# Layer-0 scan of a two-layer Macaron model: the product with B and the sum over states, made per channel half or for both halves at once on GpSimd

## The reference, cut to what matters

```python
dt = softplus(dt @ dt_proj_w + dt_proj_b)        # (8, 512, 256)
A  = -exp(A_log)                                 # (256, 16)
def step(h, inp):                                # over the 512 time steps
    u_t, dt_t, B_t, C_t = inp
    dA = exp(dt_t[..., None] * A)
    h = dA * h + (dt_t * u_t)[..., None] * B_t[:, None, :]
    y = einsum('bdn,bn->bd', h, C_t)             # sum over the 16 states
    return h, y
out = (y + u * D) * silu(z) @ out_proj_w
```

## Time and profile before

| what | us |
|---|---|
| median of 3 runs | 1867.86 |
| profiled execution, span from first to last instruction | 1918.1 |
| stretch in which scans run | about 126 to 1004 |
| TensorE busy over the span | 1729.9 |
| VectorE busy | 1279.6 |
| GpSimd busy | 1210.5 |
| ScalarE busy | 1105.3 |

### The profile page before, as it was taken

How to read it: one execution, slowest core, us unless ns; L and a number is a source line. 1 busy time by engine, 2 the same in 40 slices (tenths; PEclk the granted TensorE clock), 3 DMA queues, 4 the chain that set the end, 5 groups by cost and what they waited for, 6 DMA issues and landing times. The chain is left out here.

```text
span 1918.1 us, 35727 instructions
## 1 busy us (share of the span) xinstructions
PE 1729.9 (90%) x12089; PEld 1502.7 (78%) x12089; DVE 1279.6 (67%) x2981; ACT 1105.3 (58%) x1953; POOL 1210.5 (63%) x1201
## 2 busy tenths in 40 slices
PE   7998998999999899976779988899899999988889
PEld 6887776778878688765668867777899999877777
DVE  2358988888888987889894355334576766554333
ACT  3476766667676576756655452433677777542332
POOL 4248787787868778798985243565455555444554
PEclk9999999999999999998989999999899999989999
DMA  5023433323333233232224110113544554001113
GB/s 147 1 85 104 114 100 101 95 94 105 96 110 97 86 104 108 98 89 84 94 61 118 32 37 29 45 43 104 159 130 120 148 157 124 2 33 33 42 43 104
DMA packets 121486, 166.74 MB, mean 87 GB/s; under 512 B 14710, under 2 KB 56732, under 8 KB 121308
## 3 DMA queue, kind: packets, MB, share of 16 engines
q1 hardware_dynamic: 114268, 148.86, 25.7%
q0 software_dynamic: 7040, 15.60, 2.6%
HBM read 114.20 MB, written 50.20 MB: 86 GB/s over the span
## 5 line engine op out<-in xcount | busy, mean ns | idle before, releaser
L833 POOL TENSOR_TENSOR db<-du_m,bt 128x512 f32<-128x512 f32 x256 | 329.3, 1288 | 116.7 <-DVE bank L838 115.9
L838 DVE TENSOR_TENSOR_SCAN bank<-bank,db 128x512 f32<-128x512 f32 x256 | 312.6, 1221 | 18.2 <-ACT bank L823 17.7
L864 POOL TENSOR_TENSOR y_m<-y_m,ph 128x512 f32<-128x512 f32 x240 | 312.8, 1303 | 2.0 <-DVE ph L853 2.0
L823 ACT ACTIVATE bank<-dt_m,a_neg 128x512 f32<-128x512 f32 x256 | 176.3, 689 | 85.7 <-DVE ph L853 78.9
L853 DVE TENSOR_TENSOR ph<-bank,ct 128x512 f32<-128x512 f32 x240 | 165.9, 691 | 9.4 <-POOL y_m L864 1.1
L1355 POOL TENSOR_TENSOR s_a<-s_a,mx_a 128x768 f32<-128x768 f32 x64 | 94.1, 1470 | 87.1 <-DVE mx_a L1438 87.0
L1469 PE MATMUL bank<-vb_a,pT_a 96*128 96x64 f32 x1024 | 121.7, 272 | 0.0
L1469 PEld LDWEIGHTS bank<-vb_a,pT_a 96*128 96x128 f32 x1024 | 119.8, 193 | 0.0
L375 PEld LDWEIGHTS bank<-dn,hf1b 128*128 128x128 f32 x680 | 90.2, 194 | 16.1 <-DVE x_all L437 6.8
L375 PEld LDWEIGHTS bank<-dn,hf2b 128*128 128x128 f32 x680 | 90.2, 195 | 16.0 <-DVE x_all L437 8.3
L375 PEld LDWEIGHTS bank<-dn,hf0b 128*128 128x128 f32 x688 | 90.4, 193 | 12.0 <-DVE x_all L437 2.8
(11 more groups left out here) (480 smaller groups left out, 4877.1 us busy)
## 6 DMA issues: line engine op xcount, KB each, us to landing
bt<-bc_rows SPq DMA_DIRECT2D x128, 256.0 KB, 3.4
ct<-bc_rows SPq DMA_DIRECT2D x128, 256.0 KB, 3.4
sorted<-zero_row SPq DMA_DIRECT2D x64, 288.0 KB, 4.0
k_strips_a<-k_rows SPq DMA_DIRECT2D x32, 256.0 KB, 3.0
q_strips_a<-q_rows SPq DMA_DIRECT2D x32, 256.0 KB, 4.0
q_rows<-q_hi_a SPq DMA_DIRECT2D x16, 256.0 KB, 3.0
q_rows<-q_lo_a SPq DMA_DIRECT2D x16, 256.0 KB, 3.3
k_rows<-k_hi_a SPq DMA_DIRECT2D x16, 256.0 KB, 3.2
```

The lines of the kernel that those rows point to most:

```text
L823: eng.activation(DH[J % 2][:], dt[s % 2][:, j % NH, :], ACT.Exp, scale=a_neg[:, j % NH, j // NH:j // NH + 1]).then_inc(da_done.sem)
L833: eng.tensor_tensor(db[J % RD][:], du[s % 2][:, j % NH, :], bt[N % RB][:], ALU.mult).then_inc(db_done.sem)
L838: eng.tensor_tensor_scan(DH[J % 2][:], DH[J % 2][:], db[J % RD][:], 0.0, ALU.mult, ALU.add).then_inc(hs_done.sem)
L864: eng.tensor_tensor(y[s % 2][:, j % NH, :], y[s % 2][:, j % NH, :], ph[J % RP][:], ALU.add).then_inc(ys_done.sem)
```

## The change

The GpSimd work of two neighbouring slots (the two channel halves of one state) becomes one instruction on 128x1024: `times_b(N)` multiplies both halves of `du` by the same `bt`, read twice by a broadcast, and `ysum(N)` adds both halves. N is the state number over all sequences, so there are 128 products and 120 sums where there were 256 and 240. The buffers become pairs: `db` 2 pairs for 4 singles, `ph` 2 pairs for 3 singles. `times_b(N)` waits for the scan of slot 2N-3, that is the second half of pair N-2, and stands in GpSimd's slot 2N-3; `ysum(N)` waits for the second half's product with C and stands in slot 2N+3. Both now stand in odd slots. To pay for the memory, the tile `ones_f` goes and `sg` serves in its place at the start. VectorE, ScalarE and TensorE have the same instructions as before.

```diff
-    NJ, RP, RB, RD = NST * NH, 3, 3, 4
+    NJ, RP, RB, RD = NST * NH, 2, 3, 2
-    ph = [sb(f"ph{r}", [P, SEQ]) for r in range(RP)]
+    ph = [sb(f"ph{r}", [P, NH, SEQ]) for r in range(RP)]
-    db = [sb(f"db{r}", [P, SEQ]) for r in range(RD)]
+    db = [sb(f"db{r}", [P, NH, SEQ]) for r in range(RD)]
...
                 if N >= RB:
-                    eng.wait_ge(db_done.sem, db_done.at(NH * (N - RB) + 1))
+                    eng.wait_ge(db_done.sem, db_done.at(N - RB))
...
-        eng.memset(ones_f[:], 1.0).then_inc(zeroed.sem)
+        eng.memset(sg[0:LO + 1, 0, :], 1.0).then_inc(zeroed.sem)
...
-            if 0 <= v - LAG < END and (v - LAG) % NJ >= NH:
-                ysum(eng, v - LAG)
-            if 0 <= v + 3 < END:
-                times_b(eng, v + 3)
+            if 0 <= v - LAG < END and (v - LAG) % NJ >= NH and (v - LAG) % NH == NH - 1:
+                ysum(eng, (v - LAG) // NH)
+            if 0 <= v + 3 < END and (v + 3) % NH == 0:
+                times_b(eng, (v + 3) // NH)
...
-            eng.wait_ge(*summed(s * NJ + NJ - NH + h))
+            eng.wait_ge(*summed(s * NST + NST - 1))
...
-        if J >= RD:
-            eng.wait_ge(hs_done.sem, hs_done.at(J - RD))
+        if N >= RD:
+            eng.wait_ge(hs_done.sem, hs_done.at(NH * (N - RD) + NH - 1))
         eng.wait_ge(b_ld[N % RB].sem, b_ld[N % RB].at(N // RB))
-        eng.tensor_tensor(db[J % RD][:], du[s % 2][:, j % NH, :], bt[N % RB][:], ALU.mult).then_inc(db_done.sem)
+        eng.tensor_tensor(db[N % RD][:], du[s % 2][:], bt[N % RB][:, None, :].to_broadcast([P, NH, SEQ]), ALU.mult).then_inc(db_done.sem)
...
-            if J >= RP and (J - RP) % NJ >= NH:
-                eng.wait_ge(*summed(J - RP))
-            out = ph[J % RP][:]
+            if N >= RP and (N - RP) % NST >= 1:
+                eng.wait_ge(*summed(N - RP))
+            out = ph[N % RP][:, h, :]
...
-        eng.tensor_tensor(y[s % 2][:, j % NH, :], y[s % 2][:, j % NH, :], ph[J % RP][:], ALU.add).then_inc(ys_done.sem)
+        eng.tensor_tensor(y[s % 2][:], y[s % 2][:], ph[N % RP][:], ALU.add).then_inc(ys_done.sem)
```

More of the change, by code:

```diff
@@ L504, in mamba @@
     b_ld, c_ld = [S.dma(f"m_b{r}_spread", END) for r in range(RB)], [S.dma(f"m_c{r}_spread", END) for r in range(RB)]
-    da_done, db_done = S.count("m_decay_done", END), S.count("m_db_done", END)
-    hs_done, ph_done, ys_done = S.count("m_scan_done", END), S.count("m_ph_done", END), S.count("m_ysum_done", NSEQ * (NJ - NH))
+    da_done, db_done = S.count("m_decay_done", END), S.count("m_db_done", NSEQ * NST)
+    hs_done, ph_done, ys_done = S.count("m_scan_done", END), S.count("m_ph_done", END), S.count("m_ysum_done", NSEQ * (NST - 1))
     td = S.count("m_tail_dve", NSEQ, ("yd0", "yd1", "go0", "go1"))
@@ L570, in pool @@
     def pool(eng):
-        eng.memset(ones_f[:], 1.0).then_inc(zeroed.sem)
+        eng.memset(sg[0:LO + 1, 0, :], 1.0).then_inc(zeroed.sem)
         eng.wait_ge(zeroed.sem, zeroed.at(0, "ones"))
-        eng.tensor_copy(ones[:], ones_f[:]).then_inc(zeroed.sem)
+        eng.tensor_copy(ones[:], sg[0:LO + 1, 0, :]).then_inc(zeroed.sem)
         eng.wait_ge(mat_ld.sem, mat_ld.at(13))
@@ L685, in prep_act @@
             if s >= 2 and h == 0:
-                eng.wait_ge(db_done.sem, db_done.at((s - 1) * NJ - 1))
+                eng.wait_ge(db_done.sem, db_done.at((s - 1) * NST - 1))
             eng.wait_ge(pd.sem, pd.at(s, f"c{h}0"))
@@ L823, in decay, with times_b @@
         eng.activation(DH[J % 2][:], dt[s % 2][:, j % NH, :], ACT.Exp, scale=a_neg[:, j % NH, j // NH:j // NH + 1]).then_inc(da_done.sem)
[L825 to L828, removed]
+    def times_b(eng, N):
+        s, n = divmod(N, NST)
+        if n == 0:
             eng.wait_ge(pq.sem, pq.at(s, "du1"))
[L830 to L831 removed]
+        if N >= RD:
+            eng.wait_ge(hs_done.sem, hs_done.at(NH * (N - RD) + NH - 1))
         eng.wait_ge(b_ld[N % RB].sem, b_ld[N % RB].at(N // RB))
[L833 removed]
+        eng.tensor_tensor(db[N % RD][:], du[s % 2][:], bt[N % RB][:, None, :].to_broadcast([P, NH, SEQ]), ALU.mult).then_inc(db_done.sem)
     def scan(eng, J):
         eng.wait_ge(da_done.sem, da_done.at(J))
[L837 to L838 removed]
+        eng.wait_ge(db_done.sem, db_done.at(J // NH))
+        eng.tensor_tensor_scan(DH[J % 2][:], DH[J % 2][:], db[J // NH % RD][:, J % NH, :], 0.0, ALU.mult, ALU.add).then_inc(hs_done.sem)
     def times_c(eng, J):
@@ L849, in times_c, with summed, ysum @@
         else:
-            if J >= RP and (J - RP) % NJ >= NH:
-                eng.wait_ge(*summed(J - RP))
-            out = ph[J % RP][:]
+            if N >= RP and (N - RP) % NST >= 1:
+                eng.wait_ge(*summed(N - RP))
+            out = ph[N % RP][:, h, :]
         eng.tensor_tensor(out, DH[J % 2][:], ct[N % RB][:], ALU.mult).then_inc(ph_done.sem)
[L855 to L863, removed]
-        eng.tensor_tensor(y[s % 2][:, j % NH, :], y[s % 2][:, j % NH, :], ph[J % RP][:], ALU.add).then_inc(ys_done.sem)
+    def summed(N):
+        s, n = divmod(N, NST)
+        return ys_done.sem, ys_done.at(s * (NST - 1) + n - 1)
+    def ysum(eng, N):
+        s, n = divmod(N, NST)
+        eng.wait_ge(ph_done.sem, ph_done.at(NH * N + NH - 1))
+        if n >= 2:
+            eng.wait_ge(*summed(N - 1))
+        eng.tensor_tensor(y[s % 2][:], y[s % 2][:], ph[N % RP][:], ALU.add).then_inc(ys_done.sem)
     def pe(eng):
```

2 lines of the change are left out of this document (1 added, 1 removed).

## The result

The changed kernel takes 1907.39 us (median of 4 runs, 1906.93 to 1907.74), the kernel before 1867.58 us beside it (1866.92 to 1868.22): a ratio of 1.0211, 95% interval 1.0197 to 1.0226. That is 40 us more, where I had forecast 14 and a range that ended at 1896. The direction was right, the size was not.

What follows compares the result with a forecast made beforehand. PE and DVE were taken to hand the lead to each other, POOL full but ahead. Longer holds of 4 + 13 + 5 + 5 = 27 us on DVE, 10 + 4 passing on, gave 1882 us from 1867.9; range 1863 to 1896.

Steps and rivals of the forecast that it cites:

- The paired instruction: GpSimd's 128x1024 product or sum in the scan: 2.38 us each, ends 1.90 and 2.58.
- the second `u`: VectorE's `u` in slot 20: finds POOL idle, 0.7 us less, in the six sequences where F's router follows.
- `pick` of F: F's router in slot 21: `pick` and its `mk` held 2.2 us longer in each of six sequences, 13 us.
- `y + u*D`: Two VectorE instructions in slot 1: 3.2 us against 2.6, +0.6 in 8 sequences, 5 us.
- A's `pick` and `mk`: A's router in changing slots: `mk` put at 5 us, doubling with the instruction's length, so +5 us.
- The rings: Waits on two pairs of buffers in the scan: both fit, the second by 0.9 us; value zero, ends zero and +14 us.
- GpSimd's saving: 50 us less POOL work from pairing in the scan, counted as zero because DVE waited for POOL 1.1 us in all.
- So of 2.6 us in a sequence about 1.6 pass on: Slots 19 to 21: DVE's idle time behind the router, 1.1 us in the mean, absorbs the rest; 6 x 1.6 = 10 us.
- the other 11 us: DVE delay (1.5 + 5 + 5) falling where PE leads as often: a third counted, 4 us.
- Nothing to measure: Rival: port given back inside POOL's instruction, or PE's lead swallows the 27 us; within 0.2%, 1868; chance 0.20.
- The rings bind: Rival: buffer reserve used up in dense stretches, DVE waits for POOL; 14 us on top of 14, 1896; chance 0.09.
- Side jobs meet an idle POOL: Rival: `u`, `y + u*D` and router come late enough after odd scans to escape holds; 1851; chance 0.14.

Runs made afterwards that it cites:

- base: The kernel before, unchanged, run for a second trace: 1870.45 us, last scan starting at 1001.2 us.
- base_delay2: Kernel before plus 22.0 us of unneeded VectorE maxima behind the held instructions (slots 1, 19, start of 22): ratio 1.0083 to the kernel before.
- after_late: Changed kernel with each paired product one slot later in GpSimd's order, behind the norm work, same waits: ratio 1.0131 to the kernel before.
- base_best: Kernel before with `u` of slots 19 and 20 between scan and product with C, slot 21's product waiting for slot 22's scan: 1853.87 us, ratio 0.9905.
- after_late22: `after_late` with the product that stood with slot 21 waiting for the scan of slot 22: ratio 1.0057 to the kernel before.
- sum_only: Kernel before with only the sum over the states paired, products left single: ratio 1.0075 to the kernel before.
- after_best: Changed kernel with the edits of `base_best` and `after_late` together: ratio 1.0017 to the kernel before.
- base_ph: Kernel before with each product waiting for the multiplication by C of slot J-4, not its scan: ratio 1.0015 to the kernel before.
- base_delay: Kernel before plus 22.1 us of unneeded VectorE maxima ahead of the held instructions in slots 19, 1 and 21: ratio 1.0021 to the kernel before.

## Why the prediction was wrong

**Right: that VectorE is held longer, and by how much in all.** The paired instruction was put at 2.38 us and takes 2.375 and 2.398; the estimate from the Trainium skill (GPSIMD Engine Reference, section 3.1), 2.25 us, was 5% low. The first `u` was put at 2.4 and takes 2.37; `pick` at 1.9 and takes 1.85; the `mk` near 2 and take 2.08; the second `u` is free in most sequences. By groups, against `base`: `pick` of F +8.2 and its `mk` +6.6 (13 forecast), `y + u*D` +4.2 (5), A's `pick` and `mk` +2.1 (5), `u` +1.7 (4; I had credited the second `u` with 0.7 us, its rows give 1.25 - 0.68 = 0.57). `sel` and L332 beside it, which I left as they are, +3.9. The sum is 26.8 us where 27 were forecast, and VectorE's busy time up to the last scan rose by the same 26.8. That the sum agrees so closely is luck: `sel` and L332, put at nothing, make up for `u` and A's router, which I put too high. The rule that whoever comes first keeps the port (the Trainium skill, SBUF — State Buffer, "Who interferes with whom") is borne out at 2.38 us a piece; the last section has a case in which an instruction that came first lost. The rings were put at zero and cost at most the 3.8 us that VectorE waits for sums, GpSimd's saving at zero and it is zero.

**Wrong: the share on the path.** The step that failed was "So of 2.6 us in a sequence about 1.6 pass on", with a third counted of the other 11 us: 14 us of 27. I took the first idle time of VectorE behind the router as slack that a delay can eat. `base_delay2` shows that it isn't: 21.5 us net of VectorE work, most of it behind the router, moved the last scan by 20.4. The idle time met first does get shorter, but it comes back later. In 100 to 1000 us VectorE's waits, first `base`:

```profile
DVE x_all L437 <- PE bank L375: 68.6, 47, 5.7
...
DVE xdb L758 <- ACT xdb L705: 9.6, 4, 4.5
```

and the changed kernel:

```profile
DVE x_all L437 <- PE bank L375: 75.0, 49, 7.3
...
DVE xdb L758 <- ACT xdb L705: 4.5, 1, 4.5
```

The wait at L758, on which I had counted, shrank by 5.1 us, and the waits for the down products grew by 6.4. PE had waited for VectorE meanwhile: at L662, for L758, 12.5 us in all where `base` has 3.5. (At L653, for `u`, it waited less, 16.6 us for 20.8; that sign of mine was wrong.) My reading is that PE handed the delay back with its next down product; no run isolates that. VectorE's idle time up to the last scan didn't fall at all: 1001.2 - 808.3 = 192.9 us in `base`, 1037.4 - 835.1 = 202.3 with the change. With full passage the sum would have been +27 us, 1895, just inside the range.

**Missed: the order on GpSimd.** I had asked which wait lies ahead of the scan, and not what stands *behind* a paired product in GpSimd's own queue. A product that waits for a later scan and then lasts 2.34 us holds up A's norm, and through it ScalarE, PE and VectorE. `after_late`, which changes this alone and leaves the held sum as it is, puts it at 7.9 us.

**Missed: TensorE's clock.** The sum had no term for it. TensorE needed 16.2 us more for the same matmuls up to the last scan, at a granted clock of 0.95 for 0.97. In the second sequence the clock fell at 196.9 us, just behind TensorE's wait for VectorE, and at 207.2, within the next one. In `base_delay2`, where only work on VectorE was added, the mean clock falls as well, to 0.96, so at least part of its fall follows from a delay of VectorE. No run holds the clock fixed, and how many of the 36.2 us it carries is not known.

Together 26.8 + 7.9 = 34.7 of the 36.2 us, if the holds pass on whole. That rests on `base_delay2` (0.95), `base_best` (16.2 of held sum, 13.9 of last scan, but `u` moved too), `after_late22` (26.6, 19.6) and `sum_only` (12.7, 13.7), which put the passage between 0.74 and 1.08; the second term rests on one run. The sum's closeness proves less than it seems.

**Rivals.** *Nothing to measure* fell: the port isn't given back inside an instruction (`u` lasts 2.37 us), and VectorE's idle time did not absorb the delay. *The rings bind* fell by 3.8 us of waiting, though its 1896 came closer to the result than the forecast did. *Side jobs meet an idle POOL* holds for the second `u` alone. With slots and waits chosen for it, as in `after_best`, the change draws nearly level with the kernel before, but nearly the same choice serves single instructions better. (The forecast's own range began at 1873; the 7 us written beside it give 1875.)

**Open.** In `after_late22` the held sum is that of `base` and the last scan 8.7 us later. VectorE waits there 5.8 us for GpSimd's sums (L852 and L808), where `base` shows no such wait, and TensorE is busy 3.5 us longer; that this is the whole of it is not shown. And two runs of the kernel before don't fit a full passage: `base_ph` holds VectorE for 6.9 us more and `base_delay` burdens it with 5.8 net, at 0.1 us less and 1.0 us more of the last scan. So the passage depends on which instructions carry the delay; it was measured whole only for delays that stand where `base_delay2` puts them, in slots 1, 19 and 22.

## What to carry to other kernels

Before merging operations on GpSimd, look not for the instruction's length but for the unbroken stretch of its work, and list every VectorE instruction with two SBUF operands that will fall into it; here the time saved on an engine with time to spare bought nothing, while each hold was paid by an engine that had little. Where two engines hand the lead to each other, do not read the first idle time behind a delay as slack: put filler behind the suspected place (not ahead of it, where a hold swallows it) and measure what arrives. And look at what is queued behind an instruction that waits longer, on its own engine, however small it is.

## What the runs showed of the hardware

- A VectorE instruction can lose several times in a row. In the trace of before, a `sel` issued 0.58 us before the end of GpSimd's instruction lasts 4.29 us, through three more of them, though it is free at 0.19:

```profile
972.00 4.29 DVE L329 TENSOR_TENSOR selb<-lgb,topb 128x32 f32<-128x32 f32 x1
```

```profile
971.30 1.28 POOL L833 TENSOR_TENSOR db<-du_m,bt 128x512 f32<-128x512 f32 x1
972.54 1.27 POOL L864 TENSOR_TENSOR y_m<-y_m,ph 128x512 f32<-128x512 f32 x1
973.77 1.26 POOL L833 TENSOR_TENSOR db<-du_m,bt 128x512 f32<-128x512 f32 x1
974.99 1.26 POOL L864 TENSOR_TENSOR y_m<-y_m,ph 128x512 f32<-128x512 f32 x1
```

- It goes both ways: where VectorE is first, GpSimd's instruction lasts longer by 0.4 us, 2.80 for 2.38 us at 193.29 in the changed kernel, 1.64 for 1.29 in `base_best`.
- Filler on VectorE ahead of a held instruction was nearly free: 22.1 us of it cost 1.0 us of the front, while the held sum fell by 16.3.
- TensorE's clock fell to its lower level right behind a wait for VectorE of 2.24 us, and four matmuls took 3.59 us for 1.98.
